# ScalarE copies a tile's tokens into the attention's PSUM bank in place of a product with the identity

## The chip, the cores and the metric

One core of one Trainium2 chip. The metric is the device time of one execution in microseconds (us). The kernel is timed in several runs, of which the median counts; one further execution is recorded by the hardware profiler.

## What is computed

Two layers on 16 x 256 = 4096 tokens of 128 numbers, all f32. Each layer adds an attention part and a feed-forward part to its input, both from the normalised tokens:

```
xn = _layernorm(x, axis=-1)
x = x + _L0_attn_ref(xn, ...) + _L0_ffn_ref(xn, ...)
xn = _layernorm(x, axis=-1)
x = x + _L1_attn_ref(xn, ...) + _L1_ffn_ref(xn, ...)
return x
```

The attention of layer 0 is a causal linear attention with 16 heads of 8 (rotary positions, phi = elu + 1). A step adds k v^T to a running state KV and k to a running K_sum, takes q KV and divides it by q K_sum; the result Y goes through `Y @ Wo.T`. The feed-forward part of layer 0 is a mixture of 8 experts (128 to 512 to 128, GELU), of which each token takes two. Layer 1 has a linear attention without the causal mask and a gated feed-forward part.

## The kernel before, in words

The tokens lie in SBUF as `x_sb`, 32 tiles of 128 tokens (token on the partition). First layer 0's inputs are projected and rotated and the tokens are sorted by expert into 71 slots of 128 rows (until about 75 us of the trace). Then comes the joint loop that this document is about, and last the eight groups of layer 1 (from about 297 us).

The joint loop is written out by `steps`, in the same order for TensorE and for ScalarE. Each of its steps is one expert slot s:

- TensorE (`expert_tensor`): transpose the gathered tokens of slot s + 2 (line 487), the four up products of slot s + 1 (L497), a place in between for attention, then the down products of slot s with the bias first (L507, L509).
- ScalarE (`expert_scalar`): copy the transposed tokens (`xgT_copy`, L518), four GELUs of slot s + 1 (`gelu`, L526), the place in between, then the out copy of slot s (`out_copy`, L535, tile `ye`).
- GpSimd (POOL) gathers the tokens of a slot (L462) and scatters a slot's result (L469); SyncE loads the weights.

The attention of a tile i fills the places in between. `even(i)` and `odd(i)` stand in two slots one after the other, so that a tile takes two slots; behind tiles 15, 20 and 25 there are one or two slots more, with nothing in between (`SUMS_AT`, `READY_AT`). In even(i) TensorE projects tile i - 2 (`attn_project`, L661 and L662) and forms the cumulative products of tile i (`attn_cumsum`, L611 and L612; six for an even tile, twelve for an odd one), and ScalarE copies the projected tile back to `x_sb` (`attn_x`, L666). In odd(i) TensorE transposes y of tile i - 1 (`attn_transpose`, L649), and ScalarE copies it to SBUF (`attn_yT`, L655) and then rounds the outer products of tile i + 2 (`attn_high`, L589, tile `high`, 128x1152).

VectorE works through the tiles in order, some instructions of 1152 columns each: the outer products (L579, `outer`), the apply on the cumulative sums (L621, tile `cq`), the sums over a head (L628), the division, and the rest of the outer products after rounding (L595, `low`).

PSUM bank 5 belongs to this part of attention alone. One after the other it takes the transpose of y, and after ScalarE has copied that out, the sum of the projection and the tile's own tokens, which a product with the identity adds:

```
pe.wait_ge(yT_ready, i + 1)
nc.tensor.matmul(ps[5][:, 0:D], yT0, wT[:, 0, :], start=True, stop=False)
nc.tensor.matmul(ps[5][:, 0:D], ident, x_sb[:, ds(i, 1), :], start=False, stop=True).then_inc(o_ps, 1)
```

Every engine works through its instructions in order; semaphores (`wait_ge`, `then_inc`) order the engines among each other.

Of the kernel before, what the change touches and what calls it, by code (L numbers as in the profile page):

```python
# [8 lines left out]
D = 128  # L9
# [3 lines left out]
NT = TOK // P  # L13
# [54 lines left out]
def build(nc, x_in, Wq, Wk, Wv, Wo, Wg, bg, W1, b1, W2, b2, w_qkv, w_proj, b_proj, W_r, W_k, W_v,  # L68
# [3 lines left out]
    ds = bass.ds  # L72
    st = ExitStack()

    def sbuf(name, shape, dt=f32):
        return st.enter_context(nc.sbuf_tensor(name, shape, dt))

    def sem(name):
        return st.enter_context(nc.semaphore(name))
# [8 lines left out]
    def const(name):  # L88
        lo, hi = CONSTS[name]
        return cst[:, lo:hi]  # L90

    def passing(name):


        lo, hi = CONSTS[name]
        return cq[:, lo - NKEPT:hi - NKEPT]

    ident = const("ident")
    x_sb = sbuf("x_sb", [P, NT, D])
# [13 lines left out]
    wT = sbuf("wT", [P, 4, P])  # L113
# [64 lines left out]
    def kept(r, p):  # L178
        return 2 if r else p
# [28 lines left out]
    def row(n):  # L208
        return r32[:, n, :]

    y_tok, yT0 = sbuf("y_tok", [P, D])[:, :], sbuf("yT0", [P, P])[:, :]
# [3 lines left out]
    ps = [ps_all[:, n * 512:(n + 1) * 512] for n in range(8)]  # L215
# [32 lines left out]
        sem("outer_ready"), sem("cum_ps"), sem("cq_ready"), sem("sums_ready"), sem("y_ready"))  # L248
    rden_ready, yT_ps, yT_ready, o_ps, x_attn = (
        sem("rden_ready"), sem("yT_ps"), sem("yT_ready"), sem("o_ps"), sem("x_attn"))  # L250

    ITS = NG // 2

    def from_(g, n):

        return not isinstance(g, int) or g >= n
# [25 lines left out]
    def normalise(act, layer, g, lo=0, hi=GT):  # L282
        n = g % NB
        act.wait_ge(rstd_ready[layer], g + 1)
        if g >= NB:
            if layer == 0:
                act.wait_ge(xT_ps, g - NB + 1)
                act.wait_ge(xn_saved[n], g // NB * 16)
            else:
                act.wait_ge(xT2_ps, g - NB + 1)  # L290
        for k in range(lo, hi):
            last = nc.scalar.activation(xn[n][:, k, :], x_sb[:, g * GT + k, :], ACT.Identity,  # L292
                                        scale=rstd[g][:, k:k + 1], bias=shift[g][:, k:k + 1])
        if hi == GT:
            last.then_inc(xn_ready[layer], 1)
# [32 lines left out]
    def xT_scalar(act, g, p):  # L328
        act.wait_ge(xT_ps, g + 1)
        if from_(g, 2):  # L330
            act.wait_ge(qkv_ps, (g - 1) * 2)
        nc.scalar.copy(xT[p][:, :, :].rearrange("p a b -> p (a b)"), ps[p]).then_inc(xT_ready, 1)

    def project1_scalar(act, g, h):
        act.wait_ge(qkv_ps, g * 2 + h + 1)
        nc.scalar.copy(qkv3[:, ds(g * GT + 2 * h, 2), 2 * D:NQ],  # L336
                       ps[6 + h][:, 0:2 * NV].rearrange("p (t c) -> p t c", t=2)).then_inc(v_raw, 1)
# [245 lines left out]
    def attn_high(act, b, r, p):  # L583

        i = b * 2 + r
        act.wait_ge(outer_ready, i + 1)
        if from_(b, 2 - r):
            act.wait_ge(cum_ps, b * 2 - (0 if r else 2))
        nc.scalar.copy(high[kept(r, p)], outer[r]).then_inc(high_ready, 1)  # L589
# [61 lines left out]
    def attn_yT(act, i):  # L651
# [2 lines left out]
            act.wait_ge(o_ps, i)  # L654
        nc.scalar.copy(yT0, ps[5][:, 0:P]).then_inc(yT_ready, 1)  # L655

    def attn_project(pe, i):


        pe.wait_ge(yT_ready, i + 1)  # L660
        nc.tensor.matmul(ps[5][:, 0:D], yT0, wT[:, 0, :], start=True, stop=False)  # L661
        nc.tensor.matmul(ps[5][:, 0:D], ident, x_sb[:, ds(i, 1), :], start=False, stop=True).then_inc(o_ps, 1)  # L662

    def attn_x(act, i):
        act.wait_ge(o_ps, i + 1)
# [383 lines left out]
    with nc.Block() as block:  # L1049
# [68 lines left out]
        @block.scalar  # L1118
        def _(act):
            act.dma_start(cst[:, :], consts[:, 0:NKEPT]).then_inc(consts_in, 16)  # L1120
            for n, w in enumerate((Wq, Wk, Wv)):
                act.dma_start(w_raw[:, n, :], w).then_inc(wts_in, 16)
            act.dma_start(w_in[:, 3 * D:NQ], Wg).then_inc(wts_in, 16)
            act.dma_start(cq[:, 0:NCONST - NKEPT], consts[:, NKEPT:]).then_inc(passing_in, 16)
            act.wait_ge(wT_ps, 1)
            nc.scalar.copy(w_in[:, 0:2 * D], ps[4][:, 0:2 * P])
            nc.scalar.copy(w_in[:, 2 * D:3 * D].rearrange("p (e h) -> p h e", h=H),
                           ps[4][:, 2 * P:3 * P].rearrange("p (h e) -> p h e", e=DH)).then_inc(wT_ready, 1)
            normalise(act, 0, 0)
            xT_scalar(act, 0, 0)  # L1130
            normalise(act, 0, 1)
            for g in range(NG):
                if g + 1 < NG:
                    xT_scalar(act, g + 1, 1 - g % 2)
                project1_scalar(act, g, 0)
                if g + 2 < NG:
                    normalise(act, 0, g + 2)
                if g == 0:
                    act.wait_ge(passing_in, 16)
                    nc.scalar.copy(ones_bf[:, :], passing("ones"))  # L1140
                    nc.scalar.copy(tri_bf[:, :], passing("tri_excl"))
                    nc.scalar.copy(tri_r[:, :], passing("tri_incl"))
                    nc.scalar.copy(ones_r[:, :], passing("ones"))
                    nc.scalar.copy(tile_val[:, :, :].rearrange("p g n -> p (g n)"), passing("tile_val"))
                    nc.scalar.copy(row_mat[:, :], const("row_no").broadcast_to([P, P]))
                    nc.scalar.copy(row_no2[:, :, :], passing("iota").unsqueeze(2).broadcast_to([P, P, 2])
                                   ).then_inc(small_ready, 1)
                project1_scalar(act, g, 1)
                if g == NG - 2:
                    exp_relu(act, 0)  # L1150
            act.wait_ge(w_late_ps, 1)
            nc.scalar.copy(wT[:, 0:3, :].rearrange("p a b -> p (a b)"), ps[0][:, 0:3 * P])
            nc.scalar.activation(wT[:, 3, :], ps[0][:, 3 * P:4 * P], ACT.Copy, scale=0.5)
            nc.scalar.copy(b1T[:, :], ps[1][:, 0:NE * NC]).then_inc(w_late_ready, 1)

            for g in range(1, NG - 1):
                exp_relu(act, g)
            for g in range(NG):
                p = g % 2
                act.wait_ge(hot_ready, g + 1)  # L1160
                if g >= 2:
                    act.wait_ge(tab_ps, g - 1)
                for k in range(TOPK):
                    j = slice(k * GT // 2, (k + 1) * GT // 2)
                    last = nc.scalar.activation(hot_val[p][:, 1, j, :, :], hot_hi[p][:, j, :, :], ACT.Copy,
                                                scale=const("pair_no")[:, k:k + 1])
                last.then_inc(hot_by_row, 1)
            act.wait_ge(gate_in, 1)
            nc.scalar.activation(masked, behind, ACT.Exp)
            nc.scalar.activation(row(6), row(1), ACT.Exp).then_inc(gate_exp, 1)  # L1170
            exp_relu(act, NG - 1)

            expert = expert_of(act)

            def even(i):
                if i >= 2:
                    attn_x(act, i - 2)
                if i == NT:
                    mu_scalar(act, 0, 0)

            def last():
                act.wait_ge(pads, 3)
                xT2_copy(act, 0, 0)

            def odd(i):
                if 1 <= i <= NT:
                    attn_yT(act, i - 1)
                if i + 2 < NT:
                    attn_high(act, i // 2 + 1, i % 2, 1 - i // 2 % 2)
                if NT - 6 <= i < NT - 2:  # L1190
                    lo = i % 2 * 2
                    normalise(act, 1, (i - (NT - 6)) // 2, lo, lo + 2)
                if i == 3:
                    relu(act, NG - 1)
                if i == NT:
                    act.wait_ge(warmed, 1)
                    nc.scalar.activation(scrap["scalar"], scrap["zero"], ACT.Exp)

            def first():
                act.wait_ge(pool_const, 4)  # L1200
                nc.scalar.activation(scrap["scalar"], scrap["zero"], ACT.Gelu_apprx_tanh).then_inc(warmed, 1)
                attn_high(act, 0, 0, 0)

            def second():
                attn_high(act, 0, 1, 0)
            steps(act, lambda act, base, s, between=None: expert_scalar(act, base, s, expert, between), even, odd,
                  first=first, second=second, last=last)

            groups(act, group_scalar)
            yT1_copy(act, NG - 1)  # L1210
# [339 lines left out]
```

## Time and profile before

| | us |
|---|---|
| median of 3 runs | 381.98 |
| lowest, highest | 380.87, 382.07 |
| the profiled execution, its own time | 381.62 |
| its span in the trace | 379.5 |
| TensorE busy | 353.8 |
| VectorE busy | 330.1 |
| ScalarE busy | 264.1 |
| GpSimd busy | 233.1 |

The span runs from the first to the last instruction that the profile shows; the execution's own time is 2.1 us longer. Times inside the trace count from the span's start. Matmuls are pipelined, and their ends are modelled: the start of one to the start of the next says more than a duration. Of an f32 product the trace shows two matmuls (`x2`). TensorE had its full clock (2.4 GHz) in nearly all of the loop.

### The profile page before, as it was taken

How to read it: one execution, taken by the hardware profiler on the slowest of the kernel's cores; microseconds unless marked ns; L12 is line 12 of the kernel's file. 1: busy time of each engine (PE TensorE's matmuls, PEld its weight loads, DVE VectorE, ACT ScalarE, POOL GpSimd, SP SyncE). 2: the span in 40 equal slices, each digit the busy share in tenths (PEclk: the TensorE clock that was granted, in tenths of full speed). 3: DMA queues.
4: the chain of work that ended last, by engine and by line, in shares of the span. 5: the costliest groups of instructions: out<-in, count | busy, mean ns of one | idle time of the engine just before them, and what ended most of it. 6: DMA issues, size and time to landing. Idle time of an engine off the chain costs nothing.

```text
span 379.5 us, 9072 instructions
## 1 busy us (share of the span) xinstructions
PE 353.8 (93%) x2586; PEld 309.8 (82%) x2586; DVE 330.1 (87%) x677; ACT 264.1 (70%) x749; POOL 233.1 (61%) x240
## 2 busy tenths in 40 slices
PE   6989988699989999999999899998999999999994
PEld 2679634399989999999899899987989778888883
DVE  3787999969999999999799979996995799998663
ACT  3677987477686767676767766776784887788850
POOL 3699200688768888877888878878885433333111
PEclk9999999989999999999999999999999999999999
DMA  6832007445343555544546444446443200000001
GB/s 188 216 92 84 3 0 218 143 119 152 104 126 116 153 163 152 165 145 123 190 126 162 149 151 155 145 107 206 113 87 106 79 0 28 30 29 28 29 28 55
DMA packets 39295, 42.37 MB, mean 112 GB/s; under 512 B 5969, under 2 KB 27761, under 8 KB 39249
## 3 DMA queue, kind: packets, MB, share of 16 engines
q1 hardware_dynamic: 33840, 31.76, 28.3%
q0 software_dynamic: 4544, 9.32, 9.3%
q10 hardware_dynamic: 864, 0.73, 0.7%
q8 instruction: 23, 0.38, 0.4%
q14 instruction: 24, 0.19, 0.2%
HBM read 32.93 MB, written 8.85 MB: 110 GB/s over the span
## 4 chain that ended last, share of the span: by engine, by line
PE 66%; DVE 13%; POOL 6%; issue 6%; DMA 5%; ACT 3%; ACTq 1%; DVEq 0%
PE banks L509 13%; PE banks L497 12%; PE banks L611 5%; PE banks L612 5%; DMA xg<-xn_rows,slot_tok 4%; PE banks L900 4%; PE banks L322 3%; POOL xg L462 3%; POOL expert_rows L469 2%; PE banks L972 2%; PE banks L927 2%; PE banks L942 2%; PE banks L954 2%; PE banks L487 2%; PE banks L961 2%
## 5 line engine op out<-in xcount | busy, mean ns | idle before, releaser
L469 POOL DMA_INDIRECT expert_rows<-ye,slot_dst x71 | 97.0, 1366 | 28.1 <-issue 19.2
L462 POOL DMA_INDIRECT xg<-xn_rows,slot_tok x71 | 78.5, 1106 | 44.4 <-DVE slot_tok L1464 23.4
L526 ACT ACTIVATE xT<-banks,b1T 128x128 f32<-128x128 f32 x284 | 82.4, 385 | 26.7 <-PE banks L497 26.7
L509 PE MATMUL banks<-w_sb,xT 128*128 x568 | 79.5, 283 | 0.0
L497 PE MATMUL banks<-xgT,w 128*128 128x128 f32 x568 | 76.1, 277 | 0.0
L509 PEld LDWEIGHTS banks<-w_sb,xT 128*128 128x128 f32 x568 | 69.8, 193 | 0.8
L497 PEld LDWEIGHTS banks<-xgT,w 128*128 128x128 f32 x568 | 69.8, 194 | 0.0
L621 DVE TENSOR_TENSOR cq<-banks,phi 128x360 f32<-128x360 f32 (+1 forms) x96 | 47.5, 551 | 15.6 <-PE banks L612 15.5
L595 DVE TENSOR_TENSOR low<-outer,high 128x1152 fp32r<-128x1152 f32 x32 | 43.3, 1352 | 1.8 <-ACT high L589 1.8
L535 ACT COPY ye<-banks 128x128 f32<-128x128 f32 x71 | 19.5, 274 | 35.7 <-PE banks L509 35.7
L628 DVE TENSOR_REDUCE sums<-cq 128x144 f32<-128x1152 f32 x32 | 43.1, 1348 | 0.1
L579 DVE TENSOR_TENSOR outer<-phi,qkv 128x1152 f32<-128x1152 f32 x32 | 43.1, 1350 | 0.0
L589 ACT CAST high<-outer 128x1152 fp32r<-128x1152 f32 x32 | 37.5, 1173 | 3.8 <-DVE outer L579 2.8
L611 PE MATMUL banks<-high,tri_r 128*128 128x360 f32 (+1 forms) x96 | 35.0, 364 | 0.0
L851 POOL TENSOR_TENSOR outer<-outer,x_sb 128x512 f32<-128x512 f32 x8 | 10.2, 1272 | 40.2 <-DVE outer L846 40.2
L612 PE MATMUL banks<-low,tri_r 128*128 128x360 f32 (+1 forms) x96 | 32.3, 336 | 0.0
L300 PE MATMUL banks<-zeros_bf 128*128 128x512 bf16 x100 | 27.5, 418 | 1.7 <-DVE zeros_bf L1321 1.0
L292 ACT ACTIVATE xn<-x_sb,shift,rstd 128x128 f32<-128x128 f32 x64 | 26.8, 492 | 0.8 <-POOL shift L280 0.8
L487 PE MATMUL banks<-cst,xg 128*128 128x128 f32 x71 | 19.8, 279 | 6.0 <-DMA xg<-xn_rows,slot_tok 4.1
L322 PE MATMUL banks<-w_in,xT 128*128 128x256 f32 x64 | 19.4, 385 | 2.2 <-ACT qkv L336 1.2
L518 ACT COPY xgT<-banks 128x128 f32<-128x128 f32 x71 | 20.0, 282 | 1.4 <-PE banks L487 1.4
L300 PEld LDWEIGHTS banks<-zeros_bf 128*128 128x128 bf16 x100 | 9.9, 106 | 12.5 <-issue 4.2
(197 smaller groups left out, 733.9 us busy)
## 6 DMA issues: line engine op xcount, KB each, us to landing
w<-in_L_ffn_W SPq DMA_DIRECT2D x71, 256.0 KB
qk_exp<-expert_rows SPq DMA_DIRECT2D x8, 512.0 KB, 4.2
x_sb<-in_L_attn_x SPq DMA_DIRECT2D x8, 256.0 KB, 4.6
xn_rows<-xn SPq DMA_DIRECT2D x8, 256.0 KB, 2.3
w_sb<-in_L_ffn_W SPq DMA_DIRECT2D x8, 256.0 KB, 4.2
out<-outer SPq DMA_DIRECT2D x8, 256.0 KB, 2.3
xg<-xn_rows,slot_tok POOLq DMA_INDIRECT x71, 3.0
expert_rows<-ye,slot_dst POOLq DMA_INDIRECT x71, 3.0
```

What stands on the lines that cost most here:

```text
L462: pool.indirect_dma_start(out=xg[n][:, :], out_offset=None, in_=xn_dram, in_offset=bass.IndirectOffsetOnAxis(ap=slot_tok[:, j:j + 1], axis ...
L469: pool.indirect_dma_start(out=y_dram, out_offset=bass.IndirectOffsetOnAxis(ap=slot_dst[:, j:j + 1], axis=0), in_=ye[n][:, :], in_offset=No ...
L497: last = nc.tensor.matmul(ps[3 + p][:, c * P:(c + 1) * P], w1[n][:, c * P:(c + 1) * P], xgT[p][:, :], start=True, stop=True)
L509: last = nc.tensor.matmul(y, hidT[p][:, c, :], w2_sb[:, ds(e * NC + c, 1), :], start=False, stop=(c == NC - 1))
L526: last = nc.scalar.activation(hidT[p][:, c, :], ps[3 + p][:, c * P:(c + 1) * P], ACT.Gelu_apprx_tanh, bias=b1T[:, ds(e * NC + c, 1)])
L579: nc.vector.tensor_tensor(outer[r].rearrange("p (h e d) -> p h e d", e=E9, d=DH), k.unsqueeze(2).broadcast_to([P, H, E9, DH]), vv.unsqueez ...
L589: nc.scalar.copy(high[kept(r, p)], outer[r]).then_inc(high_ready, 1)
L595: nc.vector.tensor_tensor(low[n], outer[r], high[n].bitcast(f32), ALU.subtract).then_inc(low_ready, 1)
L611: nc.tensor.matmul(o, w[:, :], high[at][:, cols], start=(m == 0), stop=False)
L612: last = nc.tensor.matmul(o, w[:, :], low[at][:, cols], start=False, stop=(m == len(parts) - 1))
L621: last = nc.vector.tensor_tensor(cq4[:, lo:hi, :, :], ps[n][:, 0:(hi - lo) * E9 * DH].rearrange("p (h e d) -> p h e d", e=E9, d=DH), q[:, ...
L628: nc.vector.tensor_reduce(sums[:, :, :], cq4, AX.X, ALU.add).then_inc(sums_ready, 1)
```

## The change

The identity product goes. ScalarE copies the tile's tokens from `x_sb` into bank 5, after it has copied yT out of it, and raises a new semaphore `tokens_put`. The projection then waits for that semaphore and adds onto what lies in the bank. In `odd(i)` the copy stands behind `attn_yT` and `attn_high`.

```diff
+    tokens_put = sem("tokens_put")
...
+    def attn_tokens(act, i):
+        act.wait_ge(yT_ready, i + 1)
+        nc.scalar.copy(ps[5][:, 0:D], x_sb[:, i, :]).then_inc(tokens_put, 1)
+
     def attn_project(pe, i):
-        pe.wait_ge(yT_ready, i + 1)
-        nc.tensor.matmul(ps[5][:, 0:D], yT0, wT[:, 0, :], start=True, stop=False)
-        nc.tensor.matmul(ps[5][:, 0:D], ident, x_sb[:, ds(i, 1), :], start=False, stop=True).then_inc(o_ps, 1)
+        pe.wait_ge(tokens_put, i + 1)
+        nc.tensor.matmul(ps[5][:, 0:D], yT0, wT[:, 0, :], start=False, stop=True, skip_group_check=True).then_inc(o_ps, 1)
...
                     attn_yT(act, i - 1)
                 if i + 2 < NT:
                     attn_high(act, i // 2 + 1, i % 2, 1 - i // 2 % 2)
+                if 1 <= i <= NT:
+                    attn_tokens(act, i - 1)
```

On ScalarE, in one odd(i) of the loop, before: the copy of yT, the cast `high`, and then the expert's out copy (`ye`) with the next slot's copy of tokens.

```order
L655 COPY yT<-banks 128x128 [waits o_ps,yT_ps]
L589 CAST high<-outer 128x1152 [waits cum_ps,outer_ready]
L535 COPY ye<-banks 128x128 [waits ye_out2,down_ps]
L518 COPY xgT<-banks 128x128 [waits up_ps,xgT_ps]
L1045 TENSOR_LOAD slot_exp
```

And with the change (its lines are numbered one to seven higher):

```order
L656 COPY yT<-banks 128x128 [waits o_ps,yT_ps]
L590 CAST high<-outer 128x1152 [waits cum_ps,outer_ready]
L663 COPY banks<-x_sb 128x128 [waits yT_ready]
L536 COPY ye<-banks 128x128 [waits ye_out2,down_ps]
L519 COPY xgT<-banks 128x128 [waits up_ps,xgT_ps]
L1051 TENSOR_LOAD slot_exp
```

The copy of the tokens stands between the cast and the out copy, and the out copy and all behind it move back by one instruction.

On TensorE, in the even(i + 1) that follows, before: the last up products of a slot, the projection, the identity product and the cumulative products.

```order
L497 MATMUL banks<-xgT,w_2 128x128 x3
L1045 TENSOR_LOAD slot_exp
L661 MATMUL banks<-wT,yT 128x128 [waits yT_ready]
L662 MATMUL banks<-x_sb,cst 128x128
L611 MATMUL banks<-high,tri_r 128x360 [waits low_ready,cq_ready]
```

And with the change:

```order
L498 MATMUL banks<-xgT,w_2 128x128 x3
L1051 TENSOR_LOAD slot_exp
L668 MATMUL banks<-wT,yT 128x128 [waits tokens_put]
L612 MATMUL banks<-high,tri_r 128x360 [waits low_ready,cq_ready]
```

One product less, and the projection waits for `tokens_put`, which ScalarE raises one long instruction later than `yT_ready`.

## Rows read from the trace of the kernel before

**Rows 1.** The page, part 1: busy us (share of the span) and instructions per engine.
```profile
PE 353.8 (93%) x2586; PEld 309.8 (82%) x2586; DVE 330.1 (87%) x677; ACT 264.1 (70%) x749; POOL 233.1 (61%) x240
```

**Rows 2.** Busy times by stretch, 120 to 160 us, with the columns named.
```profile
core 0: us, PE busy (x) PEld busy (x) DVE busy (x) ACT busy (x) POOL busy (x), PEclk, DMA share, GB/s
120.00:160.00 40.00, 40.00 (x330) 38.62 (x329) 39.59 (x57) 28.06 (x98) 32.08 (x27) 1.00 0.53 155
```

**Rows 3.** The chain that ended last, its longest pieces: start us, us, what.
```profile
196.23 1.27 DVE low L595
...
211.81 1.27 DVE outer L579
214.90 1.06 PE banks L509 x8
```

**Rows 4.** Timeline of VectorE, an odd tile: start us, us, engine, line, operation.
```profile
125.59 1.35 DVE L595 TENSOR_TENSOR low<-outer,high 128x1152 fp32r<-128x1152 f32 x1
126.94 1.49 DVE L621 TENSOR_TENSOR cq<-banks,phi 128x360 f32<-128x360 f32 x3
```

**Rows 5.** Timeline of TensorE around one projection.
```profile
128.76 0.27 PE L649 MATMUL banks<-cst,y_tok 128*128 128x128 f32 x1
...
130.87 0.39 PE L661 MATMUL banks<-wT,yT 128*128 128x128 f32 x2
131.09 0.39 PE L662 MATMUL banks<-x_sb,cst 128*128 128x128 f32 x2
131.24 0.41 PE L611 MATMUL banks<-high,tri_r 128*128 128x360 f32 x1
```

**Rows 6.** Timeline of ScalarE at the same place, with [idle before, releaser].
```profile
129.06 1.15 ACT L526 ACTIVATE xT<-banks,b1T 128x128 f32<-128x128 f32 x4 [0.67 <-PE banks L497]
130.08 0.28 ACT L655 COPY yT<-banks 128x128 f32<-128x128 f32 x1
130.22 1.19 ACT L589 CAST high<-outer 128x1152 fp32r<-128x1152 f32 x1
131.28 0.30 ACT L535 COPY ye<-banks 128x128 f32<-128x128 f32 x1
```

**Rows 7.** Groups of ScalarE by line and shape: count, busy us, mean ns, idle before.
```profile
L292 ACT ACTIVATE xn<-x_sb,shift,rstd 128x128 f32<-128x128 f32 x64 | 26.8, 492 | 0.8 <-POOL shift L280 0.8
...
L655 ACT COPY yT<-banks 128x128 f32<-128x128 f32 x32 | 9.0, 282 | 0.3 <-PE banks L649 0.3
...
L1142 ACT CAST tri_r<-cq 128x128 fp32r<-128x128 f32 x1 | 0.3, 306 | 0.0
```

**Rows 8.** Timeline around the last projection, the one that waited for ScalarE.
```profile
299.01 0.27 ACT L655 COPY yT<-banks 128x128 f32<-128x128 f32 x1 [0.34 <-PE banks L649]
...
299.33 0.49 PE L661 MATMUL banks<-wT,yT 128*128 128x128 f32 x2
```

**Rows 9.** Timeline of TensorE and ScalarE in tiles 2 and 3 of the loop.
```profile
98.30 0.41 PE L611 MATMUL banks<-high,tri_r 128*128 128x360 f32 x1
...
100.29 0.36 PE L612 MATMUL banks<-low,ones_r 128*128 128x432 f32 x1
100.78 0.23 PE L507 MATMUL banks<-bias,ones_bf 128*128 x1
...
107.64 0.23 PE L507 MATMUL banks<-bias,ones_bf 128*128 x1 [0.97 <-ACT ye L535]
...
99.20 1.16 ACT L589 CAST high<-outer 128x1152 fp32r<-128x1152 f32 x1 [1.78 <-DVE outer L579]
```

**Rows 10.** Timeline behind tile 25, where a slot without attention follows.
```profile
250.51 0.30 ACT L535 COPY ye<-banks 128x128 f32<-128x128 f32 x1
...
251.06 0.23 PE L507 MATMUL banks<-bias,ones_bf 128*128 x1 [0.79 <-ACT ye L535]
```

**Rows 11.** Timeline of TensorE, 260 to 288 us: where it waited for a gather.
```profile
261.65 0.33 PE L487 MATMUL banks<-cst,xg 128*128 128x128 f32 x1 [1.67 <-DMA xg<-xn_rows,slot_tok]
...
281.62 0.33 PE L487 MATMUL banks<-cst,xg 128*128 128x128 f32 x1 [0.42 <-DMA xg<-xn_rows,slot_tok]
...
287.86 0.14 PEld L487 LDWEIGHTS banks<-cst,xg 128*128 128x128 f32 x1 [0.19 <-DMA xg<-xn_rows,slot_tok]
```

## The prediction

> **What bounds the kernel now.** I read the page first: TensorE (PE) is busy for 93% of the span, VectorE (DVE) for 87%, ScalarE (ACT) for 70% [rows 1]. The change touches only the joint loop of attention tiles and expert slots, so the busy times by stretch come next: in 120 to 160 us PE is busy for 40.00 of 40 us, DVE for 39.59, ACT for 28.06 [rows 2]. DVE looks as full as PE, so the chain and the timeline have to say which one waits. In the chain that ended last, `low` and `outer` cost DVE 1.27 us each, and DVE is on the chain there from about 192 to 212 us; from 214.90 on it is PE again [rows 3]. In the timeline `low` started at 125.59 and the apply behind it, which needs PE's cumulative products, at 126.94: 1.35 us on instead of 1.27 [rows 4]. In the tile before and the one behind, whose apply has another instruction ahead of it, there is no such gap. So DVE waits about 0.08 us in every two tiles and PE not at all. PE bounds, DVE is 0.08 us behind it, and **idle time put into PE's queue is added to the end**: PE has no later wait in this stretch at which it would catch up.
>
> Then the places around the change. On PE the transpose of y started at 128.76, the projection (L661) at 130.87, the identity product (L662) at 131.09, the first cumulative product (L611) at 131.24 [rows 5]. On ACT, at the same place, GELU started at 129.06 after 0.67 us of waiting for the end of PE's up products, the copy of yT at 130.08, the cast `high` at 130.22, and the next instruction, the out copy, which the change moves back, at 131.28 [rows 6]. That wait ties ACT to PE once per slot: ACT cannot run ahead.
>
> **Removed.** 32 identity products. From L661 to L662 it is 0.22 us (two passes), and an identity product takes the same: 32 x 0.22 = 7.0 us of PE work. That `start=True` becomes `start=False` in the projection costs nothing: the same passes over the same columns.
>
> **Added.** 32 ACT copies of 128x128 f32 from SBUF into PSUM. No ACT instruction of the trace writes PSUM. The neighbours: PSUM to SBUF 282 ns (L655), SBUF to SBUF with a cast 306 ns (L1142), SBUF to SBUF with scale and bias per partition 492 ns (L292) [rows 7]. I take 0.30 (source and shape of L1142, no operand per partition); the ends are 0.28 and 0.49.
> L1142's row shows what a small ScalarE copy out of SBUF costs, 306 ns. By the Trainium skill (VectorE: DVE Perf Modes, section The TRN2 errata) such a copy pays a fixed extra and takes 224 + 128 cycles, an estimate of 0.29 us: row and rule agree to 0.02 us. Against this the skill (ScalarE: Activation LUTs, Step-by-step) says that ScalarE writes PSUM faster than SBUF; no row here shows it, and by it the stall below would be a little shorter.
>
> **The new wait.** The copy stands behind `high` on ACT, and PE's projection waits for it. Count from the start of the transpose of y. ACT: GELU at +0.30, yT at +1.32, `high` at +1.46, the copy at +2.52 (where the out copy stood), its end at +2.82. Where PE once waited for ACT before a projection, yT ended at 299.28 and L661 started at 299.33, 0.05 us later, and its two passes took 0.49 instead of 0.39 [rows 5, 8]. So the projection starts at +2.87 instead of +2.11, **a stall of 0.76 us**. L611 came 0.15 us after the identity product; now it comes 0.25 after the projection, at +3.12 instead of +2.48. **0.64 us later per tile**, the saved 0.22 us already in it. In the tiles in which DVE's `outer` now holds `high` back for a moment, a later PE gives DVE the room, so they cost the same.
>
> Queued behind the waiting projection are the cumulative products, for which DVE's apply waits, and the down products, for which ACT's out copy and POOL's scatter wait. ACT has 12 of 40 us free [rows 2], so its own work does not stretch the loop further.
>
> **Which tiles.** Let i = 1 to 32 number the transposes of y. The projection comes one slot after the copy, except behind i = 15, 20 and 25, where there are one or two slots more. `high` stands ahead of the copy for i = 1 to 29.
> - i = 4 to 14, 16 to 19, 21 to 24: 19 tiles x 0.64 = 12.2 us.
> - i = 1 to 3, where DVE is late. The first gives 0.64. For i = 2 `high` started only at 99.20, when `outer` was done: the copy starts 1.06 later at 100.26 and ends at 100.56, the projection starts at 100.61 and L611 at 100.86 instead of 98.30. The last cumulative product started at 100.29 and L507 could have followed at 100.49, but was held by the out copy until 100.78; now it follows at 103.05: +2.27 [rows 9]. At i = 3 PE loses another 0.64 and gives back part of the 0.97 us that it waited at L507 [rows 9] (the same walk ends at 109.45 against 107.64): +1.8 us for the three.
> - i = 15, 20, 25: no stall at the projection, but the out copy for which PE waits at L507 (0.79 us [rows 10]) comes 0.15 later, against 0.22 saved: 3 x -0.07 = -0.2.
> - i = 26: PE waited 1.67 us for a gather before the projection [rows 11], which covers the copy: -0.2.
> - i = 27 to 29: 3 x 0.64 = 1.9, less gather waits that a later PE no longer has, 0.42 us and about 0.25 in the two behind it (0.19 in one's row) [rows 11]: +1.2.
> - i = 30: no `high` ahead, -0.2. i = 31: the copy holds up the out copy on which PE waited, +0.1. i = 32: the copy stands ahead of ACT's table load, on the chain, +0.3.
>
> Sum: 12.2 + 1.8 - 0.2 - 0.2 + 1.2 - 0.2 + 0.1 + 0.3 = **+15.0 us** on the profiled execution's 381.62 us, 396.6. The median of the runs, 381.98, lies 0.36 above that execution, so I forecast **397.0 us**. The work after the loop stays as it is.
>
> **Bounds.** Low: a stall 0.14 us shorter in every tile (19 x 0.14 = 2.7), nothing lost at i = 1 to 3 (1.8) and at 27 to 29 (1.2): 391. High: the copy at 0.49 (19 x 0.19 = 3.6): 401.
>
> **Rivals.**
> 1. *Faster: the copy is in place before PE comes.* Place: L661. The copy would have to end 0.76 us earlier than I have it, as it would ahead of `high`. Then PE saves 0.22 per tile where PE alone is on the chain, from 214.90 to 247 (5 tiles, 1.1 us); where DVE is 0.08 us behind in two tiles, 7 pairs give 0.6, and the stretch in which DVE is on the chain [rows 3] gives nothing. With 0.2 at the three wide places: 1.9 us, 380.1. Against: `high` occupies ACT for 1.06 us exactly there. 4%.
> 2. *No change: DVE bounds, and the stall hides behind it.* For: DVE's 39.59 of 40 us [rows 2]. Against: PE waits nowhere for DVE there, so DVE has nothing to give back. 382.0, 3%.
> 3. *The stall is only half felt*, because starts in the records are off by 0.3 us where engines hand over: 0.35 per tile, 19 x 0.29 = 5.5 less, 391 to 392. 11%.
> 4. *Every hand-over costs more*: a restart after 0.25 us, as from the out copy's end at 250.81 to L507 at 251.06 [rows 10], on top of a copy of 0.49: 19 x 0.39 = 7.4 more, 404. 8%.
> My forecast: 74%.
>
> **Numbers.** A measurement of this kernel tells about 0.3% (1.1 us) from no change. Slower comes from the forecast and rivals 3 and 4: 0.93; same 0.03; faster 0.04. The range takes in the forecast's bounds and rival 3, and a part of 4: 390 to 402.
>
> **What would show it.** In the profile after: PE waits at the projection for the copy, 0.76 us each, some 22 times (about 18 us in all), longest at i = 2 (near 2 us); the copy at 0.30 us, 1.06 us after `high`; two tiles in 13.6 us instead of 12.3; DVE at about 36 of 40 us in 120 to 160; smaller gather waits. No waits at the projection would prove me wrong, and so would a PE that makes up for them by shorter waits elsewhere.

## The result, and the profile after

| | before | after |
|---|---|---|
| median, us | 381.92 | 392.88 |
| lowest, highest | 380.87, 382.07 | 391.88, 393.70 |
| profiled execution, own time | 381.62 | 393.70 |
| its span | 379.5 | 391.8 |

The ratio is 1.0292, with a 95% interval from 1.0258 to 1.0327: the change makes the kernel 11.0 us slower. The forecast was 397.0, in a range from 390 to 402. The kernel before has four runs here and had three ahead of the forecast, so its median is 381.92 and not 381.98. Some runs of a kernel fall into a slower state and are left out of every ratio in this text, so a ratio can differ a little from the quotient of two medians.

The page of the kernel after, part 1, beside [rows 1]:

```profile
PE 351.9 (90%) x2522; PEld 304.4 (78%) x2522; DVE 330.0 (84%) x677; ACT 268.3 (68%) x781; POOL 237.6 (61%) x240
```

TensorE has 64 matmuls less (32 products of two passes each), ScalarE 32 instructions more, and both have lower shares of a longer span. The busy times from 120 to 160 us, with the columns of [rows 2]:

```profile
120.00:160.00 40.00, 36.45 (x284) 34.00 (x283) 35.77 (x52) 26.33 (x95) 31.51 (x25) 1.00 0.44 131
```

TensorE had 40.00 of 40 us there and now has 36.45, VectorE went from 39.59 to 35.77: nobody is full any more, which is what a wait inside the loop does. TensorE's granted clock stands at 1.00 (2.4 GHz) there before and after, so no part of this stretch's loss is a lower clock. The page's groups show who waits (busy us, mean ns, idle before):

```profile
L622 DVE TENSOR_TENSOR cq<-banks,phi 128x360 f32<-128x360 f32 (+1 forms) x96 | 47.4, 549 | 27.9 <-PE banks L613 27.9
...
L668 PE MATMUL banks<-wT,yT 128*128 128x128 f32 x64 | 15.1, 318 | 17.1 <-ACT banks L663 17.1
```

The projection (now L668) waits 17.1 us in all for ScalarE's copy of the tokens (L663), in 27 tiles. VectorE's apply, which waited 15.5 us for the cumulative products before, waits 27.9. The tile of [rows 5] and [rows 6] in the timeline of the kernel after:

```profile
131.79 0.27 PE L650 MATMUL banks<-cst,y_tok 128*128 128x128 f32 x1
...
132.09 1.14 ACT L527 ACTIVATE xT<-banks,b1T 128x128 f32<-128x128 f32 x4 [0.67 <-PE banks L498]
...
133.10 0.28 ACT L656 COPY yT<-banks 128x128 f32<-128x128 f32 x1
133.25 1.19 ACT L590 CAST high<-outer 128x1152 fp32r<-128x1152 f32 x1
...
134.30 0.30 ACT L663 COPY banks<-x_sb 128x128 f32<-128x128 f32 x1
134.50 0.30 ACT L536 COPY ye<-banks 128x128 f32<-128x128 f32 x1
134.66 0.49 PE L668 MATMUL banks<-wT,yT 128*128 128x128 f32 x2 [0.59 <-ACT banks L663]
...
134.90 0.41 PE L612 MATMUL banks<-high,tri_r 128*128 128x360 f32 x1
```

From the transpose of y at 131.79: GELU +0.30, yT +1.31, the cast +1.46, the copy +2.51, its end +2.81, the projection +2.87, the first cumulative product +3.11. The trace prints an idle of 0.59 and not 0.76, because a matmul's modelled end lies behind the point at which the next could start.

To see where the 12.3 us between the two spans lie, the transposes of y (i = 1 to 32) serve as marks. The table has the time between two marks in the timelines, for the kernels that ran on chips on which the kernel before took 380 to 382 us (380.66 beside the first four experiments, 380.06 beside the next four):

| kernel | start of i = 1 | 1 to 4 | 4 to 25 | 25 to 32 | 32 to the end | run's median |
|---|---|---|---|---|---|---|
| before | 90.20 | 19.57 | 138.22 | 50.71 | 80.80 | 381.92 |
| after | 89.77 | 21.14 | 150.19 | 49.62 | 81.08 | 392.88 |
| after, again | 87.58 | 21.14 | 150.24 | 49.73 | 81.11 | 391.96 |
| tokens ahead of the cast | 86.59 | 19.79 | 136.93 | 52.06 | 81.53 | 381.71 |
| no tokens added | 88.66 | 19.52 | 135.88 | 51.24 | 81.30 | 379.13 |
| wait, identity kept | 89.95 | 21.54 | 154.99 | 51.19 | 82.13 | 401.69 |
| copy, nobody waits | 88.18 | 19.71 | 138.57 | 50.62 | 80.92 | 380.95 |
| two copies | 86.53 | 23.15 | 154.21 | 50.95 | 81.56 | 398.60 |
| before, load later | 89.06 | 19.45 | 138.16 | 51.54 | 80.79 | 380.23 |
| after, load later | 88.14 | 21.16 | 150.20 | 49.60 | 82.10 | 392.79 |

After against before: -0.4 ahead of the loop, +1.6, +12.0, **-1.1**, +0.3. The loss lies between tiles 1 and 25, and behind tile 25 a part comes back. The two traces of the changed kernel agree within 0.03 us in every tile but one (0.12 us at i = 25).

### The profile page after: what moved, and what is told of

It reads as the page before. It is cut to its first block, busy times and chain, and to the rows that moved or that the text cites. A ratio compares the mean times of both kernels' runs of the same rounds, so it can differ in the third digit from the quotient of the medians.

```text
span 391.8 us, 8976 instructions
## 1 busy us (share of the span) xinstructions
PE 351.9 (90%) x2522; PEld 304.4 (78%) x2522; DVE 330.0 (84%) x677; ACT 268.3 (68%) x781; POOL 237.6 (61%) x240
## 4 chain that ended last, share of the span: by engine, by line
PE 76%; DVE 10%; ACT 5%; issue 5%; DMA 2%; ACTq 1%; DVEq 0%
PE banks L510 16%; PE banks L498 15%; PE banks L612 6%; PE banks L613 6%; PE banks L906 4%; PE banks L668 3%; PE banks L323 3%; ACT banks L663 2%; PE banks L978 2%; PE banks L488 2%; PE banks L933 2%; PE banks L948 2%; PE banks L960 2%; PE banks L967 2%; PE banks L940 2%
## 5 line engine op out<-in xcount | busy, mean ns | idle before, releaser
L470 POOL DMA_INDIRECT expert_rows<-ye,slot_dst x71 | 103.4, 1457 | 36.1 <-ACT ye L536 24.2
L463 POOL DMA_INDIRECT xg<-xn_rows,slot_tok x71 | 77.6, 1093 | 44.4 <-DVE slot_tok L1472 23.4
L622 DVE TENSOR_TENSOR cq<-banks,phi 128x360 f32<-128x360 f32 (+1 forms) x96 | 47.4, 549 | 27.9 <-PE banks L613 27.9
L612 PE MATMUL banks<-high,tri_r 128*128 128x360 f32 (+1 forms) x96 | 35.1, 366 | 0.0
L668 PE MATMUL banks<-wT,yT 128*128 128x128 f32 x64 | 15.1, 318 | 17.1 <-ACT banks L663 17.1
L668 PEld LDWEIGHTS banks<-wT,yT 128*128 128x128 f32 x64 | 9.5, 188 | 22.3 <-ACT banks L663 22.3
```

What stands on the lines that cost most here:

```text
L463: pool.indirect_dma_start(out=xg[n][:, :], out_offset=None, in_=xn_dram, in_offset=bass.IndirectOffsetOnAxis(ap=slot_tok[:, j:j + 1], axis ...
L470: pool.indirect_dma_start(out=y_dram, out_offset=bass.IndirectOffsetOnAxis(ap=slot_dst[:, j:j + 1], axis=0), in_=ye[n][:, :], in_offset=No ...
L612: nc.tensor.matmul(o, w[:, :], high[at][:, cols], start=(m == 0), stop=False)
L622: last = nc.vector.tensor_tensor(cq4[:, lo:hi, :, :], ps[n][:, 0:(hi - lo) * E9 * DH].rearrange("p (h e d) -> p h e d", e=E9, d=DH), q[:, ...
```

## The experiments

**Tokens ahead of the cast.** The same copy, one place earlier in ScalarE's order.

```diff
                     attn_yT(act, i - 1)
+                    attn_tokens(act, i - 1)
                 if i + 2 < NT:
                     attn_high(act, i // 2 + 1, i % 2, 1 - i // 2 % 2)
-                if 1 <= i <= NT:
-                    attn_tokens(act, i - 1)
```

> The changed kernel with ScalarE's copy of the tokens ahead of the cast instead of behind it. Theory (the whole loss is the copy's place behind the cast, 0.76 us of waiting per tile at the projection): the copy now ends about 2.0 us after the start of y's transpose, before TensorE comes at 2.11, so the waits at the projection vanish and the time falls from 392.9 to 380 to 384 us. It does not get the full 7 us of saved products, because VectorE is only 0.08 us behind in two tiles, and because the cast now starts 0.3 us later and VectorE's rest of the outer products waits for it. Rival (any hand-over of the bank from ScalarE to TensorE costs, wherever it stands): waits at the projection stay at over 0.3 us a tile and the time stays above 388.

Measured: 381.71 us, 1.004 of before (1.0009 to 1.0071). Its timeline in one tile:

```profile
126.12 0.28 ACT L656 COPY yT<-banks 128x128 f32<-128x128 f32 x1
126.43 0.27 ACT L663 COPY banks<-x_sb 128x128 f32<-128x128 f32 x1
126.64 1.15 ACT L590 CAST high<-outer 128x1152 fp32r<-128x1152 f32 x1
...
126.92 0.39 PE L668 MATMUL banks<-wT,yT 128*128 128x128 f32 x2
```

The copy ends at 126.70, TensorE comes at 126.92 and does not wait. The waits at the projection are gone but for 0.2 us in one place. So the loss belongs to the copy's place behind the cast, and a hand-over of the bank from ScalarE costs TensorE no wait by itself. The kernel is still not faster than before. Between tiles 4 and 25 it gains 1.3 us and loses 1.4 behind tile 25. Waits of its trace from 84 to 300 us:

```profile
PE banks L508 <- ACT ye L536: 8.7, 9, 1.5
ACT high L590 <- DVE outer L580: 6.2, 11, 1.8
DVE low L596 <- ACT high L590: 3.3, 7, 2.0
```

TensorE waits 8.7 us for out copies (3.9 before), and VectorE 3.3 us for the cast. It would be wrong to put all this down to the copy, which makes the cast and the out copy later on ScalarE: the next experiment has no copy at all and shows most of the first and half of the second.

**No tokens added.** Before, without the identity product and with nothing for it; layer 0's tokens are left out of the sum.

```diff
-        nc.tensor.matmul(ps[5][:, 0:D], yT0, wT[:, 0, :], start=True, stop=False)
-        nc.tensor.matmul(ps[5][:, 0:D], ident, x_sb[:, ds(i, 1), :], start=False, stop=True).then_inc(o_ps, 1)
+        nc.tensor.matmul(ps[5][:, 0:D], yT0, wT[:, 0, :], start=True, stop=True).then_inc(o_ps, 1)
```

> The kernel before without the identity product and with nothing in its place (the tokens of layer 0 are left out of the sum). This is the ceiling of what the removal can give. Theory (VectorE is the next bound at once): of 7.0 us saved on TensorE about 2 reach the end: 380 us, with VectorE busy for over 39.5 of 40 us in 120 to 160 and TensorE waiting for it. Rival (TensorE alone bounds): 375 us.

Measured: 379.13 us, 0.9974 (0.9949 to 1.0000): some 1 us, at most 2, and not 7. VectorE in its timeline, two tiles apart:

```profile
122.06 1.34 DVE L628 TENSOR_REDUCE sums<-cq 128x144 f32<-128x1152 f32 x1
...
134.27 1.34 DVE L628 TENSOR_REDUCE sums<-cq 128x144 f32<-128x1152 f32 x1
```

12.21 us for two tiles, against 12.31 before. VectorE's instructions fill that time without a gap. This is the 0.08 to 0.1 us per two tiles by which it was behind TensorE, and all that the removal can give in this stretch. The table adds where the rest goes: 2.3 us gained by tile 25, of which the last eight tiles take 0.5 back. Its waits from 84 to 300 us, beside those of the experiment before:

```profile
PE banks L507 <- ACT ye L535: 7.2, 9, 1.6
DVE low L595 <- ACT high L589: 1.6, 1, 1.6
```

TensorE's wait for out copies grows to 7.2 us without any copy of tokens on ScalarE: it is what a TensorE with less work does beside a full VectorE. What the copy ahead of the cast costs is the difference between the two experiments, 381.71 - 379.13 = 2.6 us; that the later cast and out copy are its reason is likely and not shown.

**The wait, with the identity product kept.** The changed kernel, its PE part with both products again:

```diff
         pe.wait_ge(tokens_put, i + 1)
-        nc.tensor.matmul(ps[5][:, 0:D], yT0, wT[:, 0, :], start=False, stop=True, skip_group_check=True).then_inc(o_ps, 1)
+        nc.tensor.matmul(ps[5][:, 0:D], yT0, wT[:, 0, :], start=True, stop=False)
+        nc.tensor.matmul(ps[5][:, 0:D], ident, x_sb[:, ds(i, 1), :], start=False, stop=True).then_inc(o_ps, 1)
```

> The changed kernel with the identity product kept (the projection starts the sum anew and overwrites the copied tokens), so it has the copy and the wait and saves nothing. Theory (costs add on TensorE's queue): 0.22 us per tile more than the changed kernel, 32 x 0.22 = 7 us: 400 us, and 18 us above before; each wait at the projection as in the changed kernel. Rival (a large part of the stall is hidden behind VectorE): under 396.

Measured: 401.69 us, 1.0542 (1.0506 to 1.0578), 21 us above before instead of 18. The loop, from mark 1 to mark 32, takes 227.72 us against 220.95 in the changed kernel: 6.8 us, or 0.22 for each of the 31 products between these marks, as expected. Costs on TensorE's queue add up here without loss, in the last eight tiles too: 51.19 - 49.62 = 1.57 us for seven intervals. The remaining few us lie outside the loop. The +1.0 us behind it is no effect of the edit: in the last 10 us of the span TensorE's granted clock was 0.69 of 2.4 GHz here and 0.90 in the changed kernel, and the changed kernel with the later loads (0.70) has the same 82.1 us behind the loop. The rest stays open.

**The copy, with nobody waiting.** Before, with a ScalarE copy of the identity into a spare tile in the same place (the tile's declaration is not shown).

```diff
+                if 1 <= i <= NT:
+                    nc.scalar.copy(spare, ident)
                 if NT - 6 <= i < NT - 2:
```

> The kernel before with a ScalarE copy of 128x128 f32 behind the cast, from one SBUF tile into a spare one, for which nobody waits. It has ScalarE's work of the change and not the wait. Theory (ScalarE has room; only the wait costs): 382 to 383.5 us, the rest from the out copy that comes 0.15 to 0.2 us later where TensorE waits for it (tiles 15, 20, 25) and from ScalarE's last copies. Rival (ScalarE's own work is what costs, since everything behind it is late): over 388.

Measured: 380.95 us, 1.0009 (0.9987 to 1.0031). From 4 to 25 the loop takes 0.35 us more, all of it at the two wide places in this stretch (+0.14 at i = 15, +0.20 at i = 20), where TensorE waits for the out copy. So ScalarE's work costs next to nothing here (at most 0.3%); the wait is the cost.

**The changed kernel again, and with two copies.** The second kernel has one more copy, into a spare tile, between the cast and the tokens:

```diff
+        nc.scalar.copy(spare, x_sb[:, i, :])
         nc.scalar.copy(ps[5][:, 0:D], x_sb[:, i, :]).then_inc(tokens_put, 1)
```

> The changed kernel once more, on the chip on which the runs beside it are made, as their base: 1.025 to 1.033 of the kernel before.

> The changed kernel with a second ScalarE copy of the same size between the cast and the copy of the tokens (into a spare tile). Theory (every ScalarE instruction between the cast and the token copy's end is on TensorE's path in about 24 tiles, at its start-to-start time of 0.15 to 0.2 us, not at its 0.3 us): 3.6 to 5 us above the changed kernel. Rival (each costs its full duration): 7 us above it. Rival (the stall has room): under 2 us above it.

Measured: 391.96 us, 1.0295 (1.0247 to 1.0343), and 398.60 us, 1.0497 (1.0443 to 1.0551): 6.6 us for the extra copy. That is more than the theory's 3.6 to 5 and close to the 7 of the rival by which each copy costs its full duration, so the total cannot tell them apart. The timeline of the second kernel can:

```profile
132.62 1.19 ACT L591 CAST high<-outer 128x1152 fp32r<-128x1152 f32 x1
133.68 0.33 ACT L664 COPY spare<-x_sb 128x128 f32<-128x128 f32 x1
133.88 0.30 ACT L665 COPY banks<-x_sb 128x128 f32<-128x128 f32 x1
...
134.23 0.49 PE L670 MATMUL banks<-wT,yT 128*128 128x128 f32 x2 [0.79 <-ACT banks L665]
```

The wait at the projection goes from 0.59 to 0.79: 0.20 per tile, from one copy's start to the next, and not the copy's duration of 0.33. Between the marks 4 and 25 that is 4.0 us, and behind 25 it is 1.2 us for seven tiles. Where the theory went wrong is the number of tiles: the extra copy costs 0.2 us in nearly every one, at the wide places and behind tile 25 too, and not in 24. Over the loop it is 7.2 us (228.31 against 221.11), because one tile, i = 2, added 1.60. The columns of [rows 2] for a part of that tile:

```profile
98.40:101.80 3.40, 3.40 (x15) 2.96 (x14) 1.46 (x4) 0.21 (x2) 2.08 (x2) 0.53 0.15 41
```

TensorE was granted 0.53 of its 2.4 GHz, so it ran at 1.2 GHz nearly all the time, and products of 432 columns that start 0.20 us apart in the changed kernel started 0.36 apart. Ahead of it TensorE had waited 1.83 us at the projection, as it did in that tile of the changed kernel too, where the clock stayed at 1.00. So this part belongs to this execution's clock and says nothing of the copy.

**The loads one slot later.** After tile 25 of the kernel before, TensorE waited 1.67 us for a gather [rows 11]; in the changed kernel this wait is gone. A 512 KB load had been issued shortly ahead of the gather.

```diff
-                    if j == slots_till(g) + 6:
+                    if j == slots_till(g) + 7:
```

> The kernel before with the loads of the experts' rows for the combination (512 KB each) issued one slot later. Theory (TensorE's wait of 1.67 us for a gather behind tile 25 came from the load that was issued 1.6 us ahead of the gather; in the changed kernel the load went 2 us earlier against the gather and the wait was gone, which is where 2 of my 4 us too many come from): the wait gets shorter than 0.5 us and the time falls by 1 to 2 us. Rival (it is GpSimd's lag behind TensorE, which comes from three slots without attention): the wait stays at 1 to 2 us and the time within 0.5 us.

> The changed kernel with the same loads one slot later. Theory (there is no gather wait left in it that a load could cause): within 1 us of the changed kernel. Rival (the load's place decides by itself): more than 1.5 us off, with a gather wait of over 1 us back in the trace.

Measured: 380.23 us, 0.9998 (0.9970 to 1.0026) for before, 392.79 us, 1.0317 (1.0273 to 1.0360) for the changed kernel. For before, the theory was right about the wait and wrong about the time. The gather waits did shrink, from 2.2 us in all to this:

```profile
PE banks L487 <- DMA xg<-xn_rows,slot_tok: 0.5, 1, 0.5
```

But the time stayed, and tiles 25 to 32 took 51.54 us instead of 50.71: 1.70 us were gained at i = 26 and 2.99 lost at i = 28. The chain that ended last, in that kernel, says why: from 246.02 on it runs over GpSimd, one gather or scatter after the other with 0.30 us between and one normalisation among them, until 279.88.

```profile
270.83 1.67 POOL xg L462
272.50 0.30 issue
272.80 0.99 POOL expert_rows L469
...
273.81 1.06 POOL ve L274
...
274.94 1.06 POOL rstd L276
...
276.70 1.02 POOL xg L462
```

The wait that was taken away from one gather came back at the next thing that needed GpSimd: ScalarE waited 3.61 us for `shift` (0.5 before), and TensorE 2.0 us for the out copy behind it.

**The change in some tiles only.** The first kernel of the two has the copy and the wait in the last 8 tiles, the other in the first 24; the remaining tiles are as before. Only ScalarE's side of the first is shown; TensorE's changes at the same tile.

```diff
-                if 1 <= i <= NT:
+                if 25 <= i <= NT:
                     attn_tokens(act, i - 1)
```

> The change in the last 8 of the 32 tiles only (i = 25 to 32); the first 24 have the identity product as before. Theory (GpSimd, not TensorE, sets the pace of the kernel before from tile 25 on, so TensorE's stalls there are hidden behind it): 0 to 1 us above before. Rival (my prediction's own term for this stretch, TensorE's queue alone): 1 to 2.5 us above before.

> The change in the first 24 tiles only. Theory (TensorE bounds there and every tile costs 0.64 us; 13.5 us of delay at tile 25, and then GpSimd is no longer behind, so 2 to 3 us come back that TensorE lost to it before): 10 to 12 us above before, no gather waits left. Rival (nothing is given back): 13 to 14 us above before.

> The change in the last 8 tiles only, once more, since the kernel before itself took 402 us on the chip of the first try and both traces were full of pauses that neither kernel has elsewhere. Theory (GpSimd sets the pace from tile 25 on): 0 to 1 us above before. Rival (TensorE's queue alone): 1 to 2.5 us above before.

> The change in the first 24 tiles only, once more. Theory (2 to 3 us of the 13.5 us at tile 25 come back, since GpSimd is no longer behind): 10 to 12 us above before. Rival (nothing is given back): 13 to 14 us above before.

On the chips of both tries the kernel before took 402.39 and 400.79 us, 20 us more than elsewhere, with pauses in all engines' traces, so the ratios say more than the times. Last 8 tiles: 404.09 us, 1.0006 (0.9967 to 1.0044), and 400.53 us, 0.9993 (0.9957 to 1.0028). First 24: 409.88 us, 1.0188 (1.0112 to 1.0264), and 406.89 us, 1.0157 (1.0096 to 1.0217). The cost lies in the first 24 tiles, and the last 8 show none. The intervals of the last 8 reach up to +1.8 us and +1.1 us, so they speak against the rival's 1 to 2.5 us without excluding its lower part. The first 24 came out at 6 to 8 us. The intervals reach up to 10.6 and 8.7 us, so the second lies below the 10 to 12 of the theory; on those chips I leave that open.

The traces do not bear the theory out. In neither kernel with the last 8 tiles changed does TensorE wait for a gather behind tile 25, and GpSimd is not on the chain that ended last there, although the code up to tile 25 is that of before: the pauses presumably had already made room. And of the two traces with the first 24 changed, the first has three gather waits (0.8 us in all), which the theory had excluded, and this on its chain:

```profile
286.24 2.07 POOL xg L463
288.31 0.30 issue
288.62 0.99 POOL expert_rows L470
289.61 0.30 issue
289.91 2.00 POOL xg L463
```

There TensorE reached tile 25 with the whole delay and GpSimd set the pace all the same, from 281.33 to 306.52. The second such trace has neither. So these runs say where the cost lies, and not why nothing is lost behind tile 25.

## Why the prediction was right, and where its sum was off

The direction, the mechanism and the place were right. The total alone would not say so: 391.96 and 392.88 us lie at the price of rival 3 (the stall half felt, 391 to 392) and 4 to 5 below the forecast. The marks decide between the two: 0.635 us per tile, where rival 3 has 0.35. The prediction's terms against the marks:

| term | forecast | measured |
|---|---|---|
| i = 1 to 3 | +1.8 | +1.57 |
| one tile, i = 4 to 14 | +0.64 | +0.635 (6.98 / 11) |
| i = 15 | -0.07 | -0.08 |
| i = 16 to 19 | +2.56 | +2.81 |
| i = 20 | -0.07 | -0.28 |
| i = 21 to 24 | +2.56 | +2.54 |
| from tile 25 to the last | +0.85 | **-1.09** |
| behind the loop | +0.3 | +0.28 |

- *"PE bounds, DVE is 0.08 us behind it"*: right, by the run without tokens (12.21 against 12.31 us for two tiles). With it rival 2 falls (the stall hides behind VectorE).
- *"0.64 us later per tile"*: right, and every part of the walk was. The copy took 0.306 us in the median, the projection came at +2.87, L612 at +3.11 where I had +3.12. The projection started 0.05 to 0.06 us after the copy's end in all 27 tiles in which it waited, so rival 4's dearer hand-over did not come. The 27 waits are more than the 22 that I had named, and the trace prints 24 of them as 0.59 and not 0.76.
- *The copy's price* came out at my pick, L1142's 306 ns, and the estimate of 0.29 us from the Trainium skill (VectorE: DVE Perf Modes, The TRN2 errata) is within 0.02 us of the trace. That the two agree is in part luck, for L1142 is a cast within SBUF in another surrounding. Behind the same cast `high` the experiments have plain copies of the same size into SBUF and into PSUM (ns, shortest, median and longest of 32):

```profile
L664 ACT COPY spare<-x_sb x32: 292/333/336, 89.0 to 315.4; 128x128 f32<-128x128 f32 x32
L665 ACT COPY banks<-x_sb x32: 260/305/307, 89.2 to 315.6; 128x128 f32<-128x128 f32 x32
```

  These are of the kernel with two copies; the changed kernel has 262/306/308 for its copy into PSUM, and the kernel before with a copy for which nobody waits has 290/333/337 for that one, within SBUF. So the rule that the prediction cites from the Trainium skill (ScalarE: Activation LUTs, Step-by-step) does show here, with 0.03 us per copy. The starts still lie 0.20 us apart for either.
- *i = 16 to 19* cost 0.25 more than forecast, all of it at i = 18 (+0.92 us), where GELU started 0.58 us after the transpose instead of 0.30; why is open.
- *i = 20* gave back 0.28 us, because before, the cast started 0.29 us late there (0.15 of it printed as waiting for `outer`) and the out copy with it. I had written that this wait goes away, but had not carried it into this term.
- *i = 26 to 32* is the step that was off, by 1.9 us: the terms "i = 26: -0.2" and "i = 27 to 29: 3 x 0.64 less the gather waits: +1.2". The marks have -1.25 for i = 26 and +0.53 for i = 27 to 29. I took TensorE for the bound in all the loop, and the gather waits for small gaps in its queue. But in the kernel before, the chain from 247 to 285 us runs over GpSimd. Some pieces of it, start and length:

```profile
247.35 0.97 POOL xg L462
248.32 0.30 issue
248.62 1.17 POOL expert_rows L469
...
253.24 1.06 POOL xg L462
254.30 0.30 issue
254.60 1.03 POOL expert_rows L469
255.63 0.30 issue
255.94 5.67 DMA xg<-xn_rows,slot_tok
...
273.52 1.17 POOL ve L274
...
280.29 5.19 DMA xg<-xn_rows,slot_tok
```

The same chain in the kernel after holds no GpSimd piece and no gather from 248 us on, only TensorE's products and ScalarE's copies in between; some of the latter:

```profile
263.81 0.31 ACT ye L536
264.12 0.24 issue
274.30 0.31 ACT banks L663
281.61 0.32 ACT banks L663
```

And GpSimd's waits over the whole trace, before and then after:

```profile
POOL expert_rows L469 <- ACT ye L535: 8.9, 8, 3.2
```

```profile
POOL expert_rows L470 <- ACT ye L536: 24.2, 32, 2.9
```

GpSimd waits 15 us longer for the others: it has the slack now. The 1.67 us wait and its successors vanish, and the stretch runs at TensorE's pace, 49.6 to 49.7 us in the three traces of the changed kernel (one of them with the later loads). The kernel before and its variants take 50.6 to 52.1 us there, those that reach tile 25 earliest (no tokens added, tokens ahead of the cast) longer than before. This much the marks and chains show. Two explanations are left: the delay that TensorE brings to tile 25, or the slower pace that its stalls give it behind tile 25. The trace with only the first 24 tiles changed, in which GpSimd sets the pace in spite of the delay, speaks for the second, but it comes from a chip with pauses; a clean run is missing. That one load's place costs this time was my later idea, and its run refuted it.

With this step at -1.1 the sum is 13.0, and 381.6 + 13.0 = 394.6; the profiled execution took 393.70. Of the 0.9 us between, 0.4 lie ahead of the loop (89.77 against 90.20), where the code is the same. The median is 0.8 us lower still; executions differ by this much before the changed code is reached.

*Rival 1* had its price right in kind (at most 1.9 us; the run without tokens gave 1.0 by the ratio). Its condition was met in the run with the copy ahead of the cast, and the kernel was still not faster (1.004 of before): the rival counted no cost for the copy itself.

## What to carry to other kernels

Moving a short instruction from a full engine to one with room cost nothing in work here and 11 us in order: look at what stands ahead of it in the other engine's queue, and walk both queues from their last common point to the place where they meet again. Where two engines are equally full, taking work from one gives only the gap to the next, here 0.1 us in 12.3. And read the chain of waits stretch by stretch: where another engine sets the pace, a delay can be free, as the 1.1 us that came back behind tile 25 show.

## What was not expected

- ScalarE instructions of 128 columns count with 0.15 to 0.20 us in a queue although their rows read 0.27 to 0.33 us; of those ahead of a hand-over only the last counts in full.
- The time from mark 25 to mark 32 falls by 1.1 us when the wait for the copy is added to TensorE's queue.
- Executions differ by up to 3.7 us ahead of the loop, in code that is the same in all these kernels (start of the first transpose of y from 86.53 to 90.20 us), which is more than most effects studied here. TensorE's granted clock goes with it in nine of the ten traces of the table: where it stood at 1.00 (2.4 GHz) from 0 to 20 and from 70 to 80 us, the loop began at 86.5 to 86.6; where it stood at 0.83 in the second stretch (1.2 GHz for a part of it), at 87.6 to 88.7; and where it stood at 0.91 in the first too, at 89.8 to 90.2. The tenth (before, load later) has 1.00 in both and began at 89.06. Differences between marks of the same loop repeat to about 0.2 us.
